# Order of three tile copies around the scores' maxima, in a cross-attention kernel on one core

## What is computed

```python
q = _heads(hidden_states @ to_q_w)
h_txt = _sdpa(q, _heads(ehs_txt @ to_k_w), _heads(ehs_txt @ to_v_w))
...
out = _merge(h_txt) + SCALE_OBJ * _merge(h_obj) + SCALE_OTH * _merge(h_oth) + SCALE_IP * _merge(h_ip)
out = out @ to_out_w + to_out_b
out = (out + residual) / RESCALE
```

## Time and profile before

| | |
|---|---|
| median of 3 runs | 1733.48 us (1733.34 to 1733.49) |
| the profiled execution | 1733.08 us, its span 1730.5 us |
| PE, PEld busy | 99%, 79% |
| DVE, ACT, POOL busy | 72%, 63%, 35% |
| mean granted TensorE clock | 0.997 of full speed |

### The profile page before, as it was taken

One profiled execution on the slowest core, in us unless ns is written; L12 is line 12 of the kernel. 1 busy time (PEld: TensorE's weight loads), 2 busy tenths in 40 slices (PEclk: granted clock), 3 DMA queues, 4 the chain that ended last, 5 costly groups with the idle time before them and its releaser, 6 DMA issues.

```text
span 1730.5 us, 38867 instructions
## 1 busy us (share of the span) xinstructions
PE 1706.0 (99%) x13551; PEld 1365.5 (79%) x13551; DVE 1250.5 (72%) x2525; ACT 1082.2 (63%) x5676; POOL 599.3 (35%) x814
## 2 busy tenths in 40 slices
PE   7999999999999999999999999999999999999998
PEld 7999999767777777777777777777777777777776
DVE  5222123778888888888888888888888888888874
ACT  4322123766767676776767676777767676776762
POOL 0211112433434343343434343333434343333341
PEclk9999999989999999999999999999999999999999
DMA  9544213878989889888979897979797989897965
GB/s 222 169 108 112 68 46 88 217 200 222 239 225 233 237 221 239 223 237 222 238 216 240 218 243 217 246 209 246 211 245 213 245 210 250 211 247 214 244 184 118
DMA packets 311920, 354.43 MB, mean 205 GB/s; under 512 B 40456, under 2 KB 196294, under 8 KB 311726
## 3 DMA queue, kind: packets, MB, share of 16 engines
q1 hardware_dynamic: 241422, 298.38, 64.8%
q10 hardware_dynamic: 66016, 40.97, 10.5%
q0 software_dynamic: 4288, 12.62, 2.1%
HBM read 173.07 MB, written 178.81 MB: 203 GB/s over the span
## 4 chain that ended last, share of the span: by engine, by line
PE 96%; ACT 2%; DVE 0%; DMA 0%; SPq 0%; issue 0%; ACTq 0%
PE p_ring L1099 32%; PE p_ring L1013 31%; PE p_scores L1022 9%; PE p_ring L1056 8%; PE p_bank L439 8%; PE p_bank L458 7%; ACT probs L779 2%; PE p_ring L458 1%; DMA x_raw<-in_L_xattn_to_k_w 0%; PE p_ring L1108 0%; SPq L262 0%; DVE neg_first L847 0%; PE p_scores L1072 0%; ACT x_t L808 0%; ACT o_t L798 0%
## 5 line engine op out<-in xcount | busy, mean ns | idle before, releaser
L742 POOL TENSOR_TENSOR probs<-probs,rsum 128x308 f32<-128x308 f32 x640 | 447.8, 702 | 436.0 <-DVE rsum L862 432.7
L1013 PE MATMUL p_ring<-x_t,wq_split 128*128 128x512 f32 x2400 | 581.5, 394 | 0.0
L1099 PE MATMUL p_ring<-o_t,wo_split 128*128 128x512 f32 x2385 | 568.4, 390 | 0.0
L1013 PEld LDWEIGHTS p_ring<-x_t,wq_split 128*128 128x128 f32 x2400 | 445.2, 188 | 146.9 <-ACT kv_out L790 52.8
L1099 PEld LDWEIGHTS p_ring<-o_t,wo_split 128*128 128x128 f32 x2385 | 446.2, 188 | 107.1 <-ACT kv_out L790 14.3
L779 ACT ACTIVATE probs<-p_scores,neg_first 128x77 f32<-128x77 f32 x1280 | 393.9, 363 | 18.8 <-DVE neg_second L850 18.8
L779 ACT ACTIVATE probs<-p_scores,neg_second 128x77 f32<-128x77 f32 x1280 | 401.5, 444 | 0.0
L779 ACT ACTIVATION_READ_ACCUMULATOR probs<-p_scores,neg_second 128x1 f32 x1280 | 374.9, 326 | 0.0
L870 DVE STREAM_TRANSPOSE turned<-probs 128x384 f32<-128x384 f32 x640 | 353.4, 554 | 26.5 <-POOL probs L742 26.2
L779 ACT ACTIVATION_READ_ACCUMULATOR probs<-p_scores,neg_first 128x1 f32 x1280 | 313.4, 245 | 0.0
L790 ACT ACTIVATE kv_out<-p_ring 128x512 f32<-128x512 f32 x79 | 47.2, 597 | 388.3 <-PE p_ring L1056 388.3
(11 more groups left out here) (48 smaller groups left out, 1186.8 us busy)
## 6 DMA issues: line engine op xcount, KB each, us to landing
p_scratch<-turned SPq DMA_DIRECT2D x158, 768.0 KB, 5.7
probs_t<-p_scratch SPq DMA_DIRECT2D x316, 256.0 KB
x_raw<-in_x ACTq DMA_DIRECT2D x124, 320.0 KB, 7.5
out<-out_blocks SPq DMA_DIRECT2D x124, 320.0 KB, 6.2
probs_t<-p_scratch SPq DMA_DIRECT2D x158, 104.0 KB
ctx_raw<-in_ctx SPq DMA_DIRECT2D x28, 256.0 KB, 7.3
k_sb<-k_scratch SPq DMA_DIRECT2D x32, 192.5 KB, 6.3
v_sb<-v_scratch SPq DMA_DIRECT2D x158, 38.5 KB
```

Of the source, the lines that this page charges most:

```text
L742: nc.gpsimd.tensor_tensor(heads_of(t), heads_of(t), rsum[:, n % 2, t, :].unsqueeze(2).to_broadcast([P, HG, N_TXT]), ALU.mult).then_inc(pro ...
L1013: last = nc.tensor.matmul(bank_of("Q", n)[:, :], wq_s[:, w, c, g * P:(g + 1) * P], x_t[:, a, c, :], start=c == 0 and i == 0, stop=c == CC ...
L1099: last = nc.tensor.matmul(bank_of("O", n)[:, :], wo_s[:, w, c, k * P:(k + 1) * P], o_t[b % 2][:, o, c, :], start=c == 0 and i == 0, stop=c ...
```

## The change

For the next even batch, the low part of chunk 12 (L12) moves on DVE from the end of position 3 to position 4, behind the output tile (P-1, Z-1) and the turn of the last chunk (Y14). L14 moves from behind the maxima M to in front of them. So three low parts, L12, L13 and L14, now stand in a row ahead of M, where there was one. On ACT the high part of chunk 14 (X14) moves from behind the copy K to in front of it. The last table, for the first pair, loses its L12 in the same way.

```diff
 SCALAR = orders(...
-                "K X14 U V S0 S1 S2 S3 S4 S5 S6 S7 D3")
+                "X14 K U V S0 S1 S2 S3 S4 S5 S6 S7 D3")
 VECTOR = orders(...
-                "P-3 M H W Z-3 R0 R1 T0 Y12 R2 T1 Q2 R3 T2 R4 T3 P-2 R5 T4 Z-2 R6 T5 Y13 Q3 R7 T6 L10 T7 L11 L12",
-                "P-1 Z-1 Y14 L13 M L14 W H R0 R1 T0 R2 T1 Q2 R3 T2 R4 T3 P0 R5 T4 R6 T5 Q3 R7 T6 T7 Z0")
+                "P-3 M H W Z-3 R0 R1 T0 Y12 R2 T1 Q2 R3 T2 R4 T3 P-2 R5 T4 Z-2 R6 T5 Y13 Q3 R7 T6 L10 T7 L11",
+                "P-1 Z-1 Y14 L12 L13 L14 M W H R0 R1 T0 R2 T1 Q2 R3 T2 R4 T3 P0 R5 T4 R6 T5 Q3 R7 T6 T7 Z0")
```

## The result

The changed kernel takes 1740.49 us (median of 6 runs), the kernel before 1733.53 us (6 runs). The ratio is 1.0042, 95% interval 1.0032 to 1.0051. The change makes the kernel about 7.0 us slower.

The account below looks back on a forecast made before the run. TensorE, busy 99%, bounds the kernel. Q3 0.76 us late against 0.19 now gives +0.57 us a pair, 14 pairs 8.0 us, added to 1733.5: 1741.5 us, range 1738.5 to 1745 (80%).

Parts of the forecast that it names:

- What can be gained: Q2's wait on TensorE for L14 at position 4: 0.19 us a pair, 14 pairs, 2.7 us at most.
- P-1 earlier by 0.53 us: Start of position 4 on DVE: without L12 ahead, P-1 starts at 973.80 instead of 974.33.
- M later by 0.69 us: Maxima on DVE: two more low parts cost 1.22 us, less the 0.53 us gained by P-1.
- The 0.10 us: DVE's copy of Q2 follows S0 by 5.03 us instead of 5.13, once L14 is gone from behind M.
- X14 is free: ACT: X14 fits in front of K with 0.19 us to spare, because Y14 ends 0.53 us earlier.
- L14's 1.23 us come from the neighbour and not from L14: DVE: GpSimd's subtraction beside L14 stretched it; in front of M it takes about 0.65 us.
- Q3 waits for the copy: TensorE at position 4: Q3 starts at +11.43 instead of +10.67, 0.76 us late; net +0.57 us a pair.
- The first pair costs nothing: Position 4 of the first pair: at about half clock, with more time than work on DVE, costed at nothing.
- A: Rival: only the removed wait for L14 counts, phase 17.63 us, kernel 1730.8 us; chance 5%.
- B: Rival: copy late by less than 0.4 us, at most 0.2 us a pair, 1732 to 1736 us; chance 7%.
- C: Rival: P-1 starts no earlier, M 1.22 us later, 1.10 us a pair, 1748.9 us; chance 5%.
- The clock rival, D: Rival: TensorE's new 0.76 us wait drops the clock to 1.2 GHz, 21 us on top, 1762 us; chance 1%.

Follow-up runs that it names:

- l11_too: Changed kernel with the low part L11 also moved from the end of the phase before to behind Y14; +15.8 us against the kernel before, ratio 1.0079 to 1.0107.
- l12_back: Changed kernel with L12 back at the end of the phase before; +8.6 us against the kernel before, ratio 1.0035 to 1.0063.
- x14_only: Kernel before with only X14 moved in front of K; +0.9 us, ratio 0.9996 to 1.0014.
- l12_only: Kernel before with only L12 moved behind Y14; -0.3 us, ratio 0.9991 to 1.0009.
- l14_back: Changed kernel with L14 behind the maxima M again; -1.3 us against the kernel before, ratio 0.9983 to 1.0000.

## Why the prediction was right

**What can be gained.** 14 pairs with 0.19 us each, 2.7 us. Both kernels without any wait at position 4 are 2.6 and 2.7 us faster than the kernel before. This held.

**P-1 earlier by 0.53 us.** It starts at +0.04, as read from the normal phase. Held: `l11_too` shows that the output projection sets this start, and `l12_back`, which has P-1 at +0.56 again, shows what it was worth. That L11 ended no later than the projection was close, and the prediction didn't look at it.

**M later by 0.69 us.** 0.68 measured: +3.97 instead of +3.29. Three L take 1.85 us, a step of 0.60 from one to the next. **S0** at +6.15 as predicted, **the end of the copy** at +11.20 (predicted +11.18). The 0.10 us that L14's going was to give back came, too: the copy follows S0 by 5.05 us instead of 5.13. The prediction had the cause right (L14 held up W, H and R0), though it named only the chain by S2 as what sets the copy.

**X14 is free.** It runs from +2.31 and K starts at +3.02. Held. For the case without cover the prediction had Q2 as late as K, 0.34 us; `x14_only` has K 0.35 us late and Q2 0.26.

**L14's 1.23 us come from the neighbour and not from L14.** In front of M the three L take 0.6 us each. Behind M it takes 1.23, 1.19 and 1.14 us (the kernel before, x14_only, l12_only) where GpSimd's subtraction starts some 4.7 us into the phase, and 0.77 (l14_back) where that starts at +4.36. In all four it ends 0.54 to 0.56 us behind GpSimd's end. The Trainium skill's rule (SBUF — State Buffer, SBUF: two separate sides), that the later of the two is blocked until the earlier ends, agrees with all four. In `l11_too` it is GpSimd that comes later: L14 runs from +3.98 to +4.66, and the subtraction that starts meanwhile at +4.36 takes 1.45 us instead of 1.29.

**Q3 waits for the copy.** The weight load follows the copy's end by 0.05 us. Here is the one term that was mis-sized: I had the matmul start 0.19 us behind the weight load and counted to +11.43, 0.76 us behind normal. After the wait the first matmul is recorded together with the weight load, at 989.07, +11.25. Counted at the weight loads Q3 is 11.25 - 10.45 = 0.80 us late, and the phase loses 0.73. The same difference stands in all four kernels in which Q3 waits: 0.80 late and 0.73 lost (changed), 0.19 and 0.10 (`l14_back`), 0.91 and 0.83 (`l12_back`), 1.40 and 1.31 (`l11_too`). So 0.07 to 0.09 us of the lateness cost nothing, and "paid in full" was a little too much. Net 0.53 us a pair instead of 0.57, 7.5 us instead of 8.0; the medians say 7.0. The predicted 1741.5 us stands 1.0 us over the measured 1740.49.

**The first pair costs nothing.** Its position 4 is 0.26 us longer, but just as long in a kernel with the old order (22.50 us), so no cost of the change is to be seen in it.

**The rivals.** A and B fell with Q3's wait, C with P-1 at +0.04. The clock rival, D, fell too. From 380 to 1720 us the granted clock (the third number from the end) is 1.00 in the changed kernel and in `l11_too`:

```profile
380.00:1720.00 1340.00, 1334.15 (x10656) 1014.75 (x10655) 1093.63 (x2260) 945.33 (x5164) 518.06 (x675) 1.00 0.86 225
```

```profile
380.00:1720.00 1340.00, 1329.40 (x10531) 1007.29 (x10530) 1089.80 (x2252) 944.24 (x5161) 520.04 (x675) 1.00 0.86 224
```

So waits of the weight loads of 0.84 us at Q3, and of 1.16 in `l11_too`, once in each pair, left the clock at 2.4 GHz, and 15 weight loads behind them take 3.27 us, as at Q2.

**What was not foreseen.** The prediction saw that the copy was just in time and what it hung on, but not that the copy could be taken from that chain by two words in the table.

## What to carry to other kernels

Moving work in front of an instruction delays the chain behind that instruction. Before moving it, follow the chain to the next place at which the busiest engine waits for it, and read how much time is to spare there. Here a wait worth 0.19 us was bought off with 0.6 us in front of the maxima, and the chain behind them had nothing left to give. Where two chains meet in one in-order queue, look for an instruction that stands behind a wait that it doesn't need (here the copy behind R2's wait for S2): to move it out can be worth more than to speed the chain up.

## What the runs showed beside it

A wait that the profile puts down to one engine need not be that engine's to its end. Q2's weight load stood 0.84 us "for K", but when K was 0.35 us later the load was only 0.26 later: the last 0.07 us or so were something else's. The chain of waits points at TensorE's own value sums, which ended behind K; no run tested that by itself.

Phases repeat to 0.05 us within an execution, while whole executions of one kernel differ by 0.3 to 3 us. In the ten profiles the start of the second pair alone differs by up to 1.2 us. So effects of 0.1 us a pair could be read from the phases where the interval of the ratio didn't tell them from nothing.
